# Graph attention on one core: the table of node rows stored in runs of four rows

## What is computed

```
h = relu(layernorm(x))                       # 8192 x 128
h = h @ W                                    # 8192 x 128
s_src, s_dst = h @ a[:128], h @ a[128:]      # one number of each for a node
e = leaky_relu(s_src[:, None] + s_dst[None, :], 0.2)
e = where(adj > 0, e, -9e15)                 # adj: 8192 x 8192 int32
out = x + softmax(e, axis=1) @ h
```

## Time and profile before

| | |
|---|---|
| median of 3 runs | 843.11 us (842.23 to 843.27) |
| profiled execution, its own time | 841.73 us |
| profiled execution, span of the core | 839.9 us |
| busy: PE, DVE, ACT, POOL | 65%, 71%, 65%, 67% |
| DMA bytes moved, mean rate | 299.21 MB, 356 GB/s |

### The profile page before, as it was taken

The page is one execution under the profiler, slowest core; times in us unless marked ns, Lnnn a source line. Parts: engine busy times, 40 slices in busy tenths (PEclk is TensorE's granted clock), DMA queues, the critical chain, the costliest instruction groups (busy, mean ns, idle before and its releaser), DMA issues.

```text
span 839.9 us, 8878 instructions
## 1 busy us (share of the span) xinstructions
PE 545.6 (65%) x1847; PEld 237.8 (28%) x1847; DVE 599.7 (71%) x2790; ACT 547.4 (65%) x374; POOL 559.8 (67%) x575
## 2 busy tenths in 40 slices
PE   4757677677676676666776655767677667666231
PEld 3642122233232222322332222323233222223231
DVE  7905457676776778876777768788797676779983
ACT  3969767767676676767676676676767666676000
POOL 3723777776677667676676775777777767767760
PEclk9889655655555666666556667665655665666555
DMA  9999999999999999999999999999999999993110
GB/s 285 419 300 316 398 398 398 400 398 401 402 402 400 403 402 402 403 400 403 401 403 400 401 401 403 398 389 396 393 391 402 392 399 383 391 396 119 31 26 5
DMA packets 75014, 299.21 MB, mean 356 GB/s; under 512 B 14986, under 2 KB 36274, under 8 KB 42192
## 3 DMA queue, kind: packets, MB, share of 16 engines
q1 hardware_dynamic: 49248, 276.84, 83.7%
q0 software_dynamic: 17024, 17.48, 6.7%
q10 hardware_dynamic: 8688, 4.33, 2.8%
HBM read 307.97 MB, written 8.59 MB: 377 GB/s over the span
## 4 chain that ended last, share of the span: by engine, by line
DMA 74%; ACT 11%; DVE 8%; issue 3%; PE 2%; SPq 1%; ACTq 0%; POOLq 0%; DVEq 0%
DMA adj_buf<-in_adj 74%; ACT mask_buf L423 9%; DVE x_all L718 3%; SPq L236 1%; ACT work L388 1%; PE banks L943 1%; PE banks L912 1%; ACT gathered L403 0%; ACT work L398 0%; DVE x_all L714 0%; PE banks L902 0%; DVE rest L578 0%; DVE words L580 0%; DVE words L576 0%; ACTq L415 0%
## 5 line engine op out<-in xcount | busy, mean ns | idle before, releaser
L327 POOL DMA_INDIRECT gathered<-table,index x512 | 510.5, 997 | 217.0 <-issue 171.5
L423 ACT ACTIVATE mask_buf<-adj_buf,minus_half 128x2048 bf16<-128x2048 int32 x256 | 511.4, 2001 | 210.9 <-DMA adj_buf<-in_adj 209.3
L943 PE MATMUL banks<-mask_buf,bit_ident 128*128 128x512 bf16 x1024 | 414.1, 552 | 147.6 <-ACT mask_buf L423 146.8
L943 PEld LDWEIGHTS banks<-mask_buf,bit_ident 128*128 128x128 bf16 x1024 | 105.3, 124 | 369.4 <-ACT mask_buf L423 225.7
L718 DVE SCALAR_TENSOR_TENSOR x_all<-gathered,weight,x_all 128x128 f32<-128x128 f32 x512 | 158.2, 349 | 9.3
L576 DVE MAX8 words<-banks 128x8 f32<-128x512 f32 x64 | 44.5, 696 | 156.3 <-PE banks L943 156.3
L941 PE MATMUL banks<-key_rows,ones_b 3*128 3x512 bf16 x64 | 33.7, 527 | 62.3 <-ACT mask_buf L423 61.8
L982 PE MATMUL banks<-x_all,one_hot 128*128 128x128 f32 x128 | 40.4, 415 | 13.8 <-DVE x_all L718 13.8
L580 DVE MAX8 words<-rest 128x8 f32<-128x512 f32 x64 | 44.5, 695 | 2.2
L311 POOL TENSOR_SCALAR work<-x_all,mv_all,rstd 128x128 f32<-128x128 f32 x32 | 27.0, 855 | 27.5 <-DVE nbias L535 13.8
L578 DVE MATCH_REPLACE8 rest<-words,banks 128x512 f32<-128x512 f32 x64 | 43.6, 681 | 0.0
(11 more groups left out here) (144 smaller groups left out, 487.6 us busy)
## 6 DMA issues: line engine op xcount, KB each, us to landing
adj_buf<-in_adj SPq DMA_DIRECT2D x256, 1024.0 KB, 21.1
gathered<-table,index POOLq DMA_INDIRECT x512, 2.5
table<-gathered ACTq DMA_DIRECT2D x4, 1040.0 KB, 15.7
out<-x_all SPq DMA_DIRECT2D x31, 128.0 KB
x_all<-in_x SPq DMA_DIRECT2D x2, 512.0 KB, 5.2
w_gathered<-table,w_index POOLq DMA_INDIRECT x16, 3.9
out<-x_all SPq DMA_DIRECT2D x2, 64.0 KB
w_ext<-in_L_gnn_W ACTq DMA_DIRECT2D x1, 64.0 KB, 3.3
```

Of the source, the lines that this page charges most:

```text
L327: nc.gpsimd.indirect_dma_start(g_view[buf][:, b, k, :], None, table, bass.IndirectOffsetOnAxis(index[:, buf, b, k:k + 1], 0), bounds_check ...
L423: nc.scalar.activation(mask_buf[:, u], adj_buf[:, u], ACT.Sign, bias=minus_half[:]).then_inc(mask_ready, 1)
L943: ins = mm(bank, bit_ident[:, h * PART_BITS + c], mask_buf[:, u, c * BIT_COLS:(c + 1) * BIT_COLS], start=False, stop=(h == PARTS - 1 and c ...
```

## The change

The nodes of each block of 512 (four tiles, one group) are put into the table in another order. Before, node 128*c + p of a block was its row 128*c + p; now it is row 4*p + c. The four rows that partition p holds of a block, which lie one behind the other in `rows_all`, then lie one behind the other in the table too, so a store writes runs of four rows, 2080 bytes, in place of runs of 520. The fraction in `key_rows` names the permuted row, j = 4*p + c, in place of 128*c + p; the decoded index therefore points at the permuted row with no further arithmetic.

```
-            nc.gpsimd.iota(key_parts[:, 0, :], [[0, 2], [1, 256]], base=0, channel_multiplier=0).then_inc(iotas, 1)
-            nc.gpsimd.iota(key_parts[:, 1, :], [[1, 2], [0, 256]], base=0, channel_multiplier=0).then_inc(iotas, 1)
+            nc.gpsimd.iota(key_parts[:, 0, :], [[0, FOUR], [1, P]], base=0, channel_multiplier=0).then_inc(iotas, 1)
+            nc.gpsimd.iota(key_parts[:, 1, :], [[1, FOUR], [0, P]], base=0, channel_multiplier=0).then_inc(iotas, 1)
...
             def store_rows(k):
                 act.wait_ge(rows_ready, (k + 1) * (FOURS // 4))
-                act.dma_start(table[k * QUARTER * P:(k + 1) * QUARTER * P, :].rearrange("(t p) n -> p t n", p=P),
-                              rows_all[:, k * QUARTER:(k + 1) * QUARTER, :]).then_inc(rows_stored[k], 16)
+                act.dma_start(table[k * QUARTER * P:(k + 1) * QUARTER * P, :].rearrange("(q p c) n -> p q (c n)", p=P, c=FOUR),
+                              rows_all[:, k * QUARTER:(k + 1) * QUARTER, :].rearrange("p (q c) n -> p q (c n)", c=FOUR)
+                              ).then_inc(rows_stored[k], 16)
...
-            done.add(v.tensor_scalar(key_tmp, key_parts[:, 0], ident[:, 0:1], 1.0 / BIT_COLS, ALU.mult, ALU.mult))
+            done.add(v.tensor_scalar(key_tmp, key_parts[:, 0], ident[:, 0:1], float(FOUR) / BIT_COLS, ALU.mult, ALU.mult))
             settled()
-            done.add(v.tensor_scalar(rest[:, 0], key_parts[:, 1], ident[:, 1:2], 256.0 / BIT_COLS, ALU.mult, ALU.mult))
+            done.add(v.tensor_scalar(rest[:, 0], key_parts[:, 1], ident[:, 1:2], 1.0 / BIT_COLS, ALU.mult, ALU.mult))
```

More of the change, by code:

```diff
@@ L286, in _ @@
                         sp.wait_ge(dn_mm, t * (TILES // 4) + j + 1)
-                        sp.dma_start(h_blk, table[bass.ts(j, 4 * P), 0:F].rearrange("(b p) f -> p b f", p=P)).then_inc(dn_h, 16)
+                        sp.dma_start(h_blk, table[bass.ts(j, 4 * P), 0:F].rearrange("(p b) f -> p b f", p=P)).then_inc(dn_h, 16)
                     sp.wait_ge(dn_o, t + 2)
```

## The result

The changed kernel takes 832.70 us (median of 4 runs, 832.59 to 833.75) against 842.78 us before (median of 4): ratio 0.9881, 95% interval 0.9867 to 0.9895, 10.1 us faster. The two profiled executions lie a little closer, 841.73 and 832.65 us; the spans are 839.9 and 830.8 us. The forecast for the median was 834.2 us, for the profiled execution 832.8.

A forecast was written before the change was run, and what follows sets the result against it. The prediction took the DMA engines to bound the kernel: 9.4 us saved on stores less 0.5 for a gap gave 8.9, so 841.7 became 832.8 us, plus 1.4 for the median 834.2; range 831.8 to 841.4 us (0.80).

The forecast's parts named there:

- DMA time is the currency: Main stage: the DMA engines are busy without a gap, so DMA work finished earlier moves the end forward by as much.
- The price of a packet: Setup's table stores: 2048 packets of 2080 bytes at 86 to 99 ns, 11.9 us in place of 21.3, saving 9.4 us.
- the middle of two lines: Setup's stores: lines from 28 or 44 ns at 520 bytes to 313 at 8192 give 11.0 or 12.7 us; 11.9 taken.
- the lower line: Store price from 28 ns at 520 bytes to 313 ns at 8192: 86 ns per 2080-byte packet, 11.0 us for all stores.
- The rival that the price goes with bytes: Setup's stores keep their 21.3 us of wall time at any run length; nothing gained, 843 us; chance 0.12.
- the one that the wide pitch makes a packet dearer than 166 ns: Stores at a pitch of 266,240 bytes fall on fewer memory channels; over 180 ns a packet, 844.8 us or more; chance 0.05.
- The 0.22 MB/us that I set against 0.418: Store rate set against the loads' rate, to dispute that runs of 520 bytes have nothing to win.
- The estimate that I took from the Trainium skill: Setup's stores: fixed cost of some 3 cycles per packet, so stores shrink by 12%, a gain of some 2.6 us.
- The stall of ACT: Second store's issue falls from 7.78 to 0.4 us; ACT's work behind it, including the masks, comes about 5.3 us earlier.
- Both together: Main stage's load stream starts at 61.4 us instead of 70.8; less 0.5 us for a gap, the gain is 8.9 us.
- the two limits: Start of the main stage's stream: DMA saving puts it at 61.4 us, loads issued after ACT's masks allow 60.5.
- The median: Whole kernel: profiled execution 841.7 less 8.9 is 832.8 us; 1.4 added for the median gives 834.2 us.

## Why the prediction was right, point by point

**DMA time is the currency.** Right. 3.98 MB more by 75 us are 9.5 us, and the spans differ by 9.1. Doubling the stores took 9 us of loading back, and with ACT as late as before the cheap stores alone were worth 6.5 us. SP's stores of 520 bytes had ACT 5 us earlier and gained nothing.

**The price of a packet.** Right in kind and nearly in size. I took 11.9 us for all stores, the middle of two lines; measured were 11.3 us of the engines' time (24.1% of 47 us), 86 ns each, which is the lower line, the one from the packets that run between loads. By wall time, 47 us less 14.71 MB at 0.418 MB/us leaves 11.8 us where 21.3 had been. The dear 42 and 62 ns of the earlier trace rows belonged to short packets: in the changed kernel the stores alone run at 1.40 MB in 4 us (56 to 60 us), 0.35 MB/us, against 0.24 and 0.17. The rival that the price goes with bytes is out, and so is the one that the wide pitch makes a packet dearer than 166 ns. The 0.22 MB/us that I set against 0.418 is the mean of all queues from 50 to 70 us; the stores alone ran at 0.24 and 0.17, which makes the point more strongly. The estimate that I took from the Trainium skill (DMA: Bandwidth & Descriptors, Why small descriptors are slow), 12% off the stores, does not agree with the trace: they lost 45% of their wall time. Nor does the least transfer for line rate that the Trainium skill names (same page, Specifications), 512 B: runs of 520 bytes, just above it, reached 0.24 MB/us alone, the loads 0.418.

**The stall of ACT.** Right that it goes and by how much: 0.40 us, masks from 56.8 (I had 56.9), the fourth store at 56.4 (56.5). I called it a limit on descriptors outstanding; the runs make it the next DMA in the same queue that waits, in eight of nine waits until 868 to 1135 packets ahead were left, in one until 380.

**Both together.** The stream began in effect at 61.3 us (75 us less 5.74 MB at 0.418 MB/us), where the sum had 61.4 and 0.5 more for a gap. The share from 50 to 60 us was 1.00, so there was hardly a gap. The fourteenth load was issued at 58.85 us (I had 58.9). ACT held back by 5 us showed that the two limits nearly meet: it cost 3.7 us at once.

**The median.** The profiled execution came out at 832.65 us where the sum gave 832.8. That is closer than the terms deserve: the prices between the rows allowed 8.6 to 10.3 us of saving, the gap of 0.5 us was hardly there, and 9.5 us of loading became 9.1 at the end. The forecast of the median added the 1.4 us by which the runs of before then shown lay above their profiled one; the changed kernel's median lies on its own. That is nearly the whole difference between 834.2 and 832.7 us.

## What to carry to other kernels

Where DMA bounds a kernel, read its setup by bytes per microsecond at full DMA share: a stretch that is busy and moves half the bytes is lost time, and it comes back nearly whole at the end (9.1 of 9.5 us here) if the work after it is waiting for DMA and the loads have been asked for. Make the runs in DRAM longer by choosing which node lies in which partition, and let the index that names a row carry the permutation; four rows of 520 bytes took 86 ns where they had taken 4 x 44. An engine's stall in a DMA's issue is a sign of the queue ahead of it, and moving it away alone gave 0 and 1.8 us here while the stores were dear, where an ACT that is not held gave 3.7 us once the engines had time to spare.

## What the runs showed of the hardware

The price of one packet between loads was 28, 47 and 83 ns at 520, 1040 and 2080 bytes, about 313 at 8192. With two queues active the engines took one packet from each in turn whatever their lengths (682 of q1 and 663 of q10, 592 and 552 after), so a store in short runs is starved by loads in long ones: 0.34 MB in 13 us, against 1.12 MB with runs of 2080. The issue of a DMA took up to 7.8 us when more than about 1000 packets stood ahead of it in its queue; of nine waits on ACT eight ended with 868 to 1135 left and one with 380. SP was held in the same way behind stores of 2048 packets, 7.39 us even for a load of 128 runs. Stores in runs of 520 bytes, alone on the engines, slowed from 0.24 to 0.17 MB/us in the course of 8 us; those of 2080 bytes did not (1.54 and 1.49 MB in 4 us each, from 56 to 64 us of the kernel with every store twice). Why is not settled. On two of the chips the loads broke off in the main stage while the DMA share fell to 0.14 (630 to 650 us of the kernel with stores from SP, 28 GB/s); what did that was not looked into.
